# Typed tables of a graph network on one core: relation products on row halves, nodes turned once and masked afterwards, biases in float32r halves, 16-bit work tables

## The reference, cut to what matters

```python
def typed_linear(inp_, W, b):
    y = jnp.einsum('ni,tio->tno', inp_, W) + b[:, None, :]
    return y[node_type, ar]
k = typed_linear(x, Wk, bk).reshape(n, h, dk)
q = typed_linear(x, Wq, bq).reshape(n, h, dk)
v = typed_linear(x, Wv, bv).reshape(n, h, dk)
k_rel = jnp.einsum('nhd,rhde->rnhe', k, rel_att)
v_rel = jnp.einsum('nhd,rhde->rnhe', v, rel_msg)
key_e = k_rel[edge_type, edge_src]
val_e = v_rel[edge_type, edge_src]
att = (q[edge_dst] * key_e).sum(-1) * rel_pri[edge_type] / jnp.sqrt(jnp.float32(dk))
```

## Time and profile before

| | us |
|---|---|
| median of 3 executions | 8833.31 |
| their range | 8825.69 to 8842.84 |
| span of the profiled execution (first to last instruction) | 8830.1 |
| TensorE busy in it | 6600.0 (75%) |
| DVE busy | 5164.4 (58%) |
| GpSimd busy | 4060.3 (46%) |
| ScalarE busy | 2234.7 (25%) |
| mean granted clock of TensorE | 0.819 |

### The profile page before, as it was taken

One profiled execution on the slowest core, in us unless ns is written; L12 is line 12 of the kernel. 1 busy time (PEld: TensorE's weight loads), 2 busy tenths in 40 slices (PEclk: granted clock), 3 DMA queues, 4 the chain that ended last, 5 costly groups with the idle time before them and its releaser, 6 DMA issues. The chain is left out here.

```text
span 8830.1 us, 116392 instructions
## 1 busy us (share of the span) xinstructions
PE 6600.0 (75%) x27378; PEld 5018.6 (57%) x27379; DVE 5164.4 (58%) x9644; ACT 2234.7 (25%) x4857; POOL 4060.3 (46%) x4373
## 2 busy tenths in 40 slices
PE   4977777774736666679999999974788885787886
PEld 2546566563525444546666666653676673666665
DVE  3138888886243333246666666665666666566666
ACT  1222222221310000123333333332333331333332
POOL 0025555552037777124444444423666661666663
PEclk9988888886857777589999999986777776677777
DMA  2247767666013333133343344332444441544443
GB/s 92 99 144 212 214 208 213 207 209 151 4 57 105 105 105 105 29 108 115 115 124 114 116 121 116 117 83 85 135 139 135 131 140 37 149 133 135 136 135 90
DMA packets 440058, 1096.42 MB, mean 124 GB/s; under 512 B 102452, under 2 KB 177296, under 8 KB 439410
## 3 DMA queue, kind: packets, MB, share of 16 engines
q0 software_dynamic: 249344, 763.23, 30.9%
q1 hardware_dynamic: 190180, 328.60, 11.1%
HBM read 1009.55 MB, written 81.94 MB: 124 GB/s over the span
## 5 line engine op out<-in xcount | busy, mean ns | idle before, releaser
L731 POOL DMA_INDIRECT st_rows<-g_table,st_stage_idx x1632 | 1558.0, 955 | 873.4 <-issue 463.6
L824 POOL DMA_INDIRECT st_rows<-kv_table,st_stage_idx x832 | 806.2, 969 | 671.1 <-PE st_psM L1167 391.2
L2385 PE MATMUL st_psM<-st_msg,st_hot 128*128 128x273 f32 x3264 | 942.6, 449 | 128.0 <-DVE st_msg L2233 102.6
L677 POOL DMA_INDIRECT st_rows<-p_table,st_stage_idx x816 | 854.3, 1047 | 302.9 <-issue 220.3
L731 POOL DMA_INDIRECT st_rows<-h_table,st_stage_idx x816 | 777.0, 952 | 244.5 <-issue 234.8
L2385 PEld LDWEIGHTS st_psM<-st_msg,st_hot 128*128 128x128 f32 x3264 | 702.9, 221 | 321.5 <-DVE st_msg L2233 91.2
L1519 DVE TENSOR_TENSOR st_pre<-st_psP,st_rows 128x512 f32<-128x512 f32 x816 | 523.5, 682 | 531.5 <-PE st_psP L1610 392.6
L1616 PE MATMUL st_psC<-st_w,st_rT 128*128 128x256 f32 x3264 | 814.7, 392 | 0.0
L1616 PEld LDWEIGHTS st_psC<-st_w,st_rT 128*128 128x128 f32 x3264 | 587.3, 190 | 373.7 <-ACT st_rT L1577 212.3
L1426 PE MATMUL st_psM<-st_rows,st_hot 128*128 128x256 f32 x1632 | 512.3, 484 | 372.5 <-DMA st_rows<-h_table,st_stage_idx 190.4
L1426 PEld LDWEIGHTS st_psM<-st_rows,st_hot 128*128 128x128 f32 x1632 | 401.3, 251 | 480.7 <-issue 331.3
(11 more groups left out here) (394 smaller groups left out, 11250.1 us busy)
## 6 DMA issues: line engine op xcount, KB each, us to landing
st_dst_row<-in_dst_row SPq DMA_DIRECT2D x310, 512.0 KB, 5.7
kv_table<-st_rows_out SPq DMA_DIRECT2D x25, 1560.0 KB, 5.7
st_ea<-in_ea SPq DMA_DIRECT2D x103, 256.0 KB, 3.8
st_rows<-g_table,st_stage_idx POOLq DMA_INDIRECT x1632, 2.8
st_pens<-pen_table SPq DMA_DIRECT2D x208, 72.0 KB
st_rows<-kv_table,st_stage_idx POOLq DMA_INDIRECT x832, 4.5
st_rows<-h_table,st_stage_idx POOLq DMA_INDIRECT x816, 2.7
st_rows<-p_table,st_stage_idx POOLq DMA_INDIRECT x816, 3.7
```

The source lines that it names most:

```text
L677: pool.indirect_dma_start(out=rows[:, u * SLOTS + j, :], out_offset=None, in_=table, in_offset=bass.IndirectOffsetOnAxis(ap=stage_idx[:, u ...
L731: pool.indirect_dma_start(out=rows[:, slot, j, :], out_offset=None, in_=table, in_offset=bass.IndirectOffsetOnAxis(ap=stage_idx[:, g, u * ...
L824: pool.indirect_dma_start(out=rows[:, slot, j, :], out_offset=None, in_=kv_table, in_offset=bass.IndirectOffsetOnAxis(ap=stage_idx[:, g, u ...
L2385: last = nc.tensor.matmul(out[:, 0:MSG_W], onehots[:, j, :], msg[:, n, j, :], start=(j == 0), stop=(j == SLOTS - 1))
```

## The change

Five things are changed, all in `typed_tables` but for the last:

- The relation products are made per head. `rel` holds only the 64x64 matrices, 64 rows per head, two heads above each other; a pair of heads is two products of 64 rows and 384 columns, on the upper and the lower row half, into two banks of `psR[c]` (0 and 512). The copies read both and write the same rows as before.
- The nodes are normalised once (`h`, with the helper `normed`) and turned once, two transposes; DVE multiplies the turned rows by `mask_rows`, each type's one-hot row on all 128 partitions, on the way to `hT`. DVE's loop is peeled like those of ScalarE and TensorE.
- The bias products take float32r. The bias is put in `b3` twice, in rows 0 to 2 rounded and in rows 32 to 34 what rounding left, with the one-hot rows in both places; 35 rows in all.
- SP's loads change with that: three loads for `mask_rows` come first, the relation matrices are loaded denser, the biases and one-hot rows twice.
- `work` and `typed_work` hold 16-bit numbers.

```diff
...
-    work = sb(top, "work", [1, NS + 2 * U + 2, 4], I32)
+    work = sb(top, "work", [1, NS + 2 * U + 2, 4], U16)
...
-    typed_work = sb(early, "typed_work", [1, NS + 2 * U + 2, 4], I32)
+    typed_work = sb(early, "typed_work", [1, NS + 2 * U + 2, 4], U16)
...
-            b3 = st.sb("b3", [TYPES, 3 * D])
-            rel = st.sb("rel", [P, 2, 2, RELS, P])
+            LOW = 32
+            BIAS = LOW + TYPES
+            b3 = st.sb("b3", [BIAS, 3 * D], F32R)
+            b_in = st.sb("b_in", [BIAS, 3 * D])
+            DK = D // H0
+            rel = st.sb("rel", [P, 2, 2, RELS, DK])
...
-            hm = st.sb("hm", [P, TYPES, D])
-            hot3 = st.sb("hot3", [TYPES, P])
+            h = st.sb("h", [P, D])
+            hot3 = st.sb("hot3", [BIAS, P], F32R)
+            mask_rows = st.sb("mask_rows", [P, TYPES, NPAD])
...
+            def head_rows(n, c):
+                return rows[:, :, n * D + c * P:n * D + (c + 1) * P].rearrange("p r (y d) -> p y r d", y=2)
+
+            def head_sums_of(c):
+                return psR[c][:, :].rearrange("p (y x) -> p y x", y=2)[:, :, 0:RELS * DK].rearrange("p y (r d) -> p y r d", r=RELS)
...
-                    sp.dma_start(type_rows[:, :], type_rows_table).then_inc(S["types_in"], 16)
+                    for t in range(TYPES):
+                        sp.dma_start(mask_rows[:, t, :], type_rows_table[t, :].partition_broadcast(P)).then_inc(S["types_in"], 16)
...
-                    for n, w in enumerate(("bq", "bk", "bv")):
-                        sp.dma_start(b3[:, n * D:(n + 1) * D], a[w]).then_inc(S["w_in"], 16)
                     sp.wait_ge(S["zeroed"], START + 1)
+                    for lo in (0, LOW):
+                        sp.dma_start(type_rows[lo:lo + TYPES, :], type_rows_table).then_inc(S["b_in"], 16)
+                        for n, w in enumerate(("bq", "bk", "bv")):
+                            sp.dma_start(b_in[lo:lo + TYPES, n * D:(n + 1) * D], a[w]).then_inc(S["b_in"], 16)
...
-                    def masked_transposed(b):
-                        act.wait_ge(S["hT_ps"], START + b + 1)
-                        nc.scalar.copy(hT[:, :, :].rearrange("p a c -> p (a c)"), psT[:, 0:6 * P]).then_inc(S["hT"], 1)
-
...
+                    def mask_turned(b):
+                        dve.wait_ge(S["hT_ps"], START + b + 1)
+                        wide = [P, TYPES, 2, P]
+                        v.tensor_tensor(hT[:, :, :].rearrange("p (t c) n -> p t c n", t=TYPES),
+                                        psT[:, :].rearrange("p (c n) -> p c n", c=2).unsqueeze(1).to_broadcast(wide),
+                                        mask_rows[:, :, ds(b * P, P)].unsqueeze(2).to_broadcast(wide), ALU.mult).then_inc(S["hT"], 1)
...
+                    dve.wait_ge(S["b_in"], 16 * 8)
+                    link(v.tensor_copy(b3[:, :], b_in[:, :]))
+                    v.tensor_tensor(b3[LOW:BIAS, :], b_in[LOW:BIAS, :], b3[LOW:BIAS, :].bitcast(F32), ALU.subtract).then_inc(S["b_ready"], 1)
+                    dve.wait_ge(S["types_in"], 16 * TYPES)
+                    mask_turned(0)
                     dve.wait_ge(S["rel_in"], 16 * 3 * H0)
...
                         v.tensor_copy(NODE[:, block_of(b), 0:D].squeeze(1), psY[:, 0:D]).then_inc(S["kv"], 1)
+                        if ahead:
+                            mask_turned(b + 1)
                         dve.wait_ge(S["stored"], START + b)
...
                         pe.wait_ge(S["hm"], START + b + 1)
-                        for q in range(2 * TYPES):
-                            last = nc.tensor.transpose(psT[:, q * P:(q + 1) * P], hm[:, q // 2, (q % 2) * P:(q % 2 + 1) * P], ident[:, :])
+                        pe.wait_ge(S["hT"], START + b)
+                        for c in range(2):
+                            last = nc.tensor.transpose(psT[:, c * P:(c + 1) * P], h[:, c * P:(c + 1) * P], ident[:, :])
...
-                                for lo, hi in ((0, 4), (4, RELS)):
-                                    last = nc.tensor.matmul(psR[c][:, lo * P:hi * P], kvT[:, 2 * n + c, :],
-                                                            rel[:, n, c, lo:hi, :].rearrange("p r d -> p (r d)"),
+                                for y in range(2):
+                                    half = slice(y * DK, (y + 1) * DK)
+                                    last = nc.tensor.matmul(psR[c][:, y * 512:y * 512 + RELS * DK], kvT[half, 2 * n + c, :],
+                                                            rel[half, n, c, :, :].rearrange("p r d -> p (r d)"),
                                                             start=True, stop=True)
...
                     transposed(0)
+                    pe.wait_ge(S["w_in"], 16 * N_W)
+                    pe.wait_ge(S["b_ready"], START + 1)
+                    pe.wait_ge(S["weights_ready"], START + 2)
```

More of the change, by code:

```diff
@@ L20 @@
 F32 = mybir.dt.float32
+F32R = mybir.dt.float32r
 BF16 = mybir.dt.bfloat16
 I32 = mybir.dt.int32
+U16 = mybir.dt.uint16
 ALU = mybir.AluOpType
@@ L532, in _ @@
                         for n, w in enumerate(("rel_att", "rel_msg")):
-                            sp.dma_start(rel[half, n, h // 2, :, half],
+                            sp.dma_start(rel[half, n, h // 2, :, :],
                                          a[w][:, h, :, :].rearrange("r d e -> d r e")).then_inc(S["rel_in"], 16)
@@ L550, in _, with normalised @@
                 def _(act):
[L551 to L557, removed]
+                    def normalised(b):
+                        act.wait_ge(S["hT_ps"], START + b)
+                        normed(act, h[:, :], b).then_inc(S["hm"], 1)
                     def types(b):
                         nc.scalar.copy(hot3[:, :], type_rows[:, ds(b * P, P)]).then_inc(S["hot"], 1)
-                    def masked_transposed(b):
-                        act.wait_ge(S["hT_ps"], START + b + 1)
-                        nc.scalar.copy(hT[:, :, :].rearrange("p a c -> p (a c)"), psT[:, 0:6 * P]).then_inc(S["hT"], 1)
                     def finish_block(b, ahead):
                         if ahead:
-                            masked(b + 1)
+                            normalised(b + 1)
                             act.wait_ge(S["qkv"], START + b + 1)
@@ L577, in finish_block @@
                             act.wait_ge(S["rel"], START + 4 * b + 2 * n + 1)
-                            nc.scalar.copy(rows[:, :, n * D:n * D + P], psR[0][:, 0:RELS * P].rearrange(
-                                "p (r d) -> p r d", r=RELS)).then_inc(S["rel_a"], 1)
-                    masked(0)
-                    act.wait_ge(S["types_in"], 16)
+                            nc.scalar.copy(head_rows(n, 0), head_sums_of(0)).then_inc(S["rel_a"], 1)
+                    normalised(0)
+                    act.wait_ge(S["b_in"], 16 * 8)
                     types(0)
-                    masked_transposed(0)
                     if NB > 1:
@@ L596, in _ @@
                         v.memset(rows[:, r, 2 * D + r:2 * D + r + 1], 1.0)
-                    for t in range(TYPES):
-                        link(v.tensor_tensor(rs3[:, t, :], rstd[:, :], type_mask[:, t, :], ALU.mult))
-                        last = v.tensor_tensor(nm3[:, t, :], nmr[:, :], type_mask[:, t, :], ALU.mult)
-                        if t < TYPES - 1:
-                            link(last)
-                    last.then_inc(S["masks"], 1)
+                    dve.wait_ge(S["b_in"], 16 * 8)
[3 more added lines that the diff above has]
+                    mask_turned(0)
                     dve.wait_ge(S["rel_in"], 16 * 3 * H0)
@@ L607, in _, with finish_block @@
                         last = v.tensor_tensor(rel[:, 0, c, :, :], rel[:, 0, c, :, :],
-                                               pri[:, c, :].unsqueeze(2).to_broadcast([P, RELS, P]), ALU.mult)
+                                               pri[:, c, :].unsqueeze(2).to_broadcast([P, RELS, DK]), ALU.mult)
                         last.then_inc(S["weights_ready"], 1)
-                    with dve.Fori(0, NB) as b:
+                    def finish_block(b, ahead):
                         dve.wait_ge(S["qkv"], START + b + 1)
```

24 lines of the change are left out of this document (11 added, 13 removed).

## The result

The changed kernel takes **9063.21 us** (median of 4 runs, 9059.34 to 9064.62) against 8832.07 (4 runs, 8825.69 to 8842.84): ratio 1.0262, 95% interval 1.0249 to 1.0274. It is slower by 231 us; 8794 and a gain had been forecast. The profiled execution has a span of 9060.9 us (before 8830.1); `typed_tables` did a little more than was forecast, and something else cost more than five times its gain.

The account below looks back on a forecast made before the run. TensorE was taken to bound typed_tables' loop (421 of 450 us busy), the one stage changed. Relation halves -45, biases -16, loads +12 and clock +10 summed to -39 us: 8794 us, range 8764 to 8828.

Parts of the forecast that it names:

- Work tables in 16 bits: Register loads from both tables: only the bytes change, taken as 0; ends -5 and +15 us.
- The rest of the kernel keeps its instructions, so what the change is worth is the change of this stage: Premise that only typed_tables, about 101 to 592 us of the span, changes the time.
- the last one: Sign of being wrong: the typed pass, behind typed_tables, changes its length by more than 5 us.
- Relation halves: typed_tables loop: row halves overlap, phase 3.5 us instead of 5.3; 1.8 us a block, -45 us.
- Biases: typed_tables loop: float32r takes one pass instead of two, 0.64 us a block, -16 us.
- Transposes, masked copy, stores: typed_tables loop: fewer transposes, masked copy moved to DVE, waits for stores landing; each worth nothing.
- Loads ahead of the loop: Before typed_tables' loop: mask loads delay the first q, k, v product to about 146; about +12 us.
- Clock: TensorE in typed_tables' loop: 8 falls to 1.2 GHz instead of 2, 1.70 us each; +10 us.
- 1 (halves one after another): Rival: relation halves don't overlap, the 45 us go; 8833 us, no change; chance 0.12.
- 3 (the clock gives it back): Rival: clock falls in each block, in some twice; some 9040 us if it stayed at 1.2 GHz; chance 0.06.
- Rival 2: Float32r and clock both kind in typed_tables: -45 - 24 + 8 + 0, 8772 us; chance 0.12.
- the 0.05 for slower: Chance given to the whole kernel getting slower; faster by over 0.2% had 0.81.

Follow-up runs that it names:

- e2: Kernel before the change with only the two work tables in 16 bits; 9166.29 us, ratio 1.0375.
- e1: Changed kernel with both work tables in 32 bits again, loop bounds masked in a register, two more store waits; 8761.52 us, ratio 0.9916.
- e8: e1 plus a 16-bit copy of typed_work that only DVE reads in the typed pass; 8920.51 us (one execution), typed pass 1689.8 us.
- e6: e1 with relation products on full 128-row blocks with zeros again, as before the change; 8805.15 us (one execution).
- e12: e2 with thirteen one-column copies added in ScalarE's program behind the square root of the statistics; 9121.37 us, ratio 1.0326.
- e11: e10 with the four priority loads at the head of SP's queue; 8755.04 us, ratio 0.9918.
- e10: e1 with only the first 128 mask-row columns loaded ahead, the rest behind the relation weights and priorities; 8752.67 us, ratio 0.9915.
- e5: e1 with a stage ahead of typed_tables where SP, DVE and TensorE load and use 16- and 32-bit numbers; 8902.14 us (one execution).

## Why the prediction was wrong

**The step that failed** is "Work tables in 16 bits ... Taken as 0; ends: -5 and +15 us". It costs some 300 us: 332 in e2, 302 between the change (9063) and e1 (8762), whose masking itself costs something; in neither pair do ScalarE's stops in the GAT passes differ. Three things were wrong in it. The price: it was bounded by "a quarter dearer", a figure that no row gave; the load became 2.8 times as dear. The row showed the time of one layout, four neighbouring 32-bit numbers, and said nothing of another; that they might be fetched one by one was a case to be bounded, and was not. The count: 308 loads, not 154 (the row has both numbers, and the forecast took that of one form). And the reach: only the typed pass was named, though `work` is loaded by DVE 476 times and by TensorE and ScalarE 612 times each behind it. The Trainium skill's 200 ns per register, cited above, would have been the rival: 308 x (0.8 - 0.344) is an estimate of 140 us for the typed pass by the Trainium skill's figure, and it measured 154 (e8 against e1) to 160 (the change against before). The sentence "The rest of the kernel keeps its instructions, so what the change is worth is the change of this stage" failed with it. Of the signs named ahead, the last one struck: the typed pass changed by 159.5 us, not by up to 5.

**The rest of the sum was about right, and a little short.** For `typed_tables` it came to -39 us; measured -51.7:
- Relation halves: -45 forecast; the phase is 3.46 us (forecast 3.5), and e6 gives 1.72 us a block, 43 in all.
- Biases: -16 forecast, 0.94 us a block and 23.5 us measured. The term was mis-sized at "one pass instead of two": between 256 and 512 columns a float32r product grows by 0.11 us (0.31 to 0.42), where one pass of float32 grows by 0.215. So it holds TensorE about half as long as one pass, 0.11 and 0.22 us, and the 0.2 us around it stay, as forecast. The estimate in the prediction by the Trainium skill, "TensorE: Matmul & The Clock Gate", Back-to-back issue gap, 0.97 a block and 24 us, was right.
- Transposes, masked copy, stores: nothing, as forecast; DVE's masked product ends at 154.36, its next need is 2.20 us later.
- Loads ahead of the loop: +12 forecast (first product at 146), +7.1 measured (140.73 against 133.67), 6.4 counted from the stage's start (101.7 against 101.0). The tail of relation and priority loads does "simply start later": it takes 18.3 us from its first issue to its last landing in both kernels (110.7 to 129.0, 120.7 to 139.0). But it starts 10.0 us later where the terms came to 15, and 2.9 us come back where 3.4 were forecast.
- Clock: +10 forecast by eight falls of 1.70 us. There are ten, of 1.1 to 1.4 us each; less the 3.4 us of before that is +8. The mean granted clock is 0.96 from 150 to 400 us, 0.99 before. The sum was right with the number of falls too low and their price too high.

-43 - 23.5 + 6.4 + 8 is -52.1, near the 51.7.

**The rivals.** 1 (halves one after another) and 3 (the clock gives it back) didn't come. Rival 2 (float32r kind) was right on its term. Rival 3 came near the measured time by luck: its 9040 us stand for a clock that stays at 1.2 GHz in the loop, and there the mean granted clock was 0.96. No rival had the loads, and so the 0.05 for slower was too little for a change that touches an operand of every pass.

**One part of e1's gain is no merit of the change.** It is 61.7 us faster than before in the profiled executions (72 in the medians): `typed_tables` -54.1, the two GAT passes -31.8, and +22.9 in the typed and edge passes, which I put down to the masking and the two waits (argued, not tried by itself). The 31.8 come with the code's place: ScalarE's stops of 88 and 106 us in the GAT passes of before are gone, and e12 shows that thirteen idle instructions do as much (44.5 us). In the change they are gone too, which hid some 41 us of its loss (its GAT passes against e2's).

**What stays open:** what holds SP up in its weight loads in the change and in e11 and not in e10; what the loop would gain if TensorE's first q, k, v products didn't wait for the relation matrices; and how near the loads of a short table could come to the one-go form in 16 bits with another packing.

## What to carry to other kernels

A load of registers is an operation of its engine's queue with a price of its own: look for the loads' duration in the source view, multiply by all of them (the count behind x, on every engine), and ask which engine has no slack. Keep four numbers that are loaded together as neighbouring 32-bit numbers; narrower tables save bytes and cost 0.6 us a load here. And before a gain or loss of 1% in an untouched loop is explained, look at the instruction queue's packets and at idle time put down to "issue": code that moved took 1.7% off the GAT passes in e12 and put 6% onto the typed pass in e5.

## What the hardware showed that was not expected

- Loads of registers (e5): 0.28 to 0.31 us for one number on DVE, 0.22 for each more, but 0.348 for four neighbouring 32-bit numbers; in steps of two places 0.950, and two neighbours 0.524.
- Code: thirteen instructions ahead of a loop took 45 us off the kernel; in e5 a stage of 26 us put 95 us of stops into another stage.
- A float32r product holds TensorE 0.42 us for 512 columns and 0.31 for 256, the two passes of float32 1.05 and 0.63 us. All four contain some 0.2 us around the product.
- Two products on the two row halves, each in two passes, run beside each other: 8 passes of 384 columns start to end in 1.56 us, where one behind the other they would take an estimated 2.6 (8 x 0.32).
